# A selective scan on one core: the z projection goes into the unit that uses it, and the order tables around the silu block are set anew

## The reference

```python
def step(h, inp):
    d_t, B_t, C_t, u_t = inp
    h = h * jnp.exp(d_t[..., None] * A) + (d_t * u_t)[..., None] * B_t[:, None, :]
    y = jnp.einsum('bcn,bn->bc', h, C_t)
    return (h, y)

def _mamba_layer(x, Wi, cw, cb, Wx, Wdt, bdt, Alog, Dp, Wo):
    xz = jnp.einsum('bld,ed->ble', x, Wi)
    xin, z = jnp.split(xz, 2, axis=-1)
    xin = _silu(_causal_conv(xin, cw, cb))
    x_dbl = jnp.einsum('blc,ec->ble', xin, Wx)      # dt_raw, Bm, Cm
    delta = jax.nn.softplus(jnp.einsum('blr,cr->blc', dt_raw, Wdt) + bdt)
    y = _selective_scan(delta, Bm, Cm, xin, A, Dp)  # the scan over time of step()
    y = y * _silu(z)
    return jnp.einsum('blc,dc->bld', y, Wo)

for i in range(DEPTH):                              # 8 layers, 16 states, 512 inner channels
    x = x + _mamba_layer(x, W_in[i], ...)
```

## Time and profile before

| | us |
|---|---|
| median of 3 runs | 7655.07 |
| range of the runs | 7652.78 to 7655.28 |
| the profiled execution | 7654.07 |
| its span, first to last instruction | 7652.3 |
| DVE busy in the span | 6625.8 (87%) |
| PE busy | 6888.8 (90%) |
| ACT busy | 6410.1 (84%) |
| POOL busy | 5895.9 (77%) |

### The profile page before, as it was taken

How to read it: one execution, slowest core, us unless ns; L and a number is a source line. 1 busy time by engine, 2 the same in 40 slices (tenths; PEclk the granted TensorE clock), 3 DMA queues, 4 the chain that set the end, 5 groups by cost and what they waited for, 6 DMA issues and landing times. The chain is left out here.

```text
span 7652.3 us, 143629 instructions
## 1 busy us (share of the span) xinstructions
PE 6888.8 (90%) x39999; PEld 4756.2 (62%) x39999; DVE 6625.8 (87%) x6510; ACT 6410.1 (84%) x10314; POOL 5895.9 (77%) x4917
## 2 busy tenths in 40 slices
PE   6979999999999999999999999999999999999997
PEld 4646666666666666666666666666666666666665
DVE  3259988988998898889889988988998898899888
ACT  1258888888888888888988888888888888888987
POOL 2148887888888788888888888888888788888875
PEclk9989999999999999999999999999999999999998
DMA  4111111111111111111111111111111111111112
GB/s 163 34 43 39 41 40 47 43 40 40 42 47 42 40 39 47 44 40 39 41 47 44 40 39 42 47 43 39 41 48 43 39 40 42 45 44 40 40 39 92
DMA packets 222613, 352.40 MB, mean 46 GB/s; under 512 B 43856, under 2 KB 78448, under 8 KB 221712
## 3 DMA queue, kind: packets, MB, share of 16 engines
q1 hardware_dynamic: 218048, 332.70, 14.8%
q0 software_dynamic: 3792, 10.38, 0.4%
HBM read 325.00 MB, written 17.98 MB: 45 GB/s over the span
## 5 line engine op out<-in xcount | busy, mean ns | idle before, releaser
L897 POOL TENSOR_TENSOR drive<-du,brep 128x512 f32<-128x512 f32 x4096 | 5537.7, 1382 | 702.9 <-DVE du L1140 461.2
L936 ACT ACTIVATE prod<-ps_r,cT 128x512 f32<-128x512 f32 x4096 | 2860.8, 700 | 344.2 <-PE ps_r L1244 341.9
L929 ACT ACTIVATE ps_d<-delta,cur 128x512 f32<-128x512 f32 x4096 | 2896.9, 710 | 252.6 <-DVE state L1090 241.4
L1244 PE MATMUL ps_r<-ident,state 128*128 128x128 f32 x16384 | 2543.4, 278 | 402.3 <-ACT prod L936 153.2
L1090 DVE TENSOR_TENSOR_SCAN state<-ps_d,carry,drive 128x512 f32<-128x512 f32 x2048 | 2500.5, 1262 | 283.6 <-ACT ps_d L929 283.4
L1090 DVE TENSOR_TENSOR_SCAN state<-ps_d,drive 128x512 f32<-128x512 f32 x2048 | 2404.4, 1206 | 329.1 <-ACT ps_d L929 309.0
L1251 PE MATMUL ps_y<-ident,prod 128*128 128x128 f32 x16384 | 2459.5, 274 | 28.1 <-ACT prod L936 25.8
L1244 PEld LDWEIGHTS ps_r<-ident,state 128*128 128x128 f32 x16384 | 1829.5, 141 | 849.9 <-ACT prod L936 416.3
L1251 PEld LDWEIGHTS ps_y<-ident,prod 128*128 128x128 f32 x16384 | 1923.4, 141 | 668.6 <-issue 584.2
L1291 PE MATMUL ps_r<-xm,w_inz_sb 128*128 128x512 f32 x1024 | 506.9, 618 | 48.6 <-ACT prod L936 48.6
L1283 PE MATMUL ps_r<-xm,w_inx_sb 128*128 128x512 f32 x1024 | 510.2, 621 | 35.7 <-ACT prod L936 28.1
(11 more groups left out here) (144 smaller groups left out, 4653.4 us busy)
## 6 DMA issues: line engine op xcount, KB each, us to landing
brep<-bc_dram SPq DMA_DIRECT2D x1024, 256.0 KB, 3.2
w_sb<-w SPq DMA_DIRECT2D x8, 1024.0 KB
w_all<-w SPq DMA_DIRECT2D x8, 1024.0 KB, 11.5
xb<-xs_dram SPq DMA_DIRECT2D x39, 128.5 KB, 2.1
w_all<-x SPq DMA_DIRECT2D x4, 1024.0 KB, 9.4
w_inx_sb<-w_in SPq DMA_DIRECT2D x8, 512.0 KB, 4.1
w_inz_sb<-w_in SPq DMA_DIRECT2D x8, 512.0 KB, 4.9
w_out_sb<-w_out SPq DMA_DIRECT2D x8, 512.0 KB, 3.9
```

The source lines that it names most:

```text
L897: nc.gpsimd.tensor_tensor(drive[:, k % DRIVE, :], du[:, j, :], brep[:, n % BREP, :], ALU.mult).then_inc(drive_set, 1)
L929: nc.scalar.activation(ps_d[:, k % 2, :], delta[h][:, j, :], ACT.Exp, scale=cur[h][:, a:a + 1]).then_inc(decay_set, 1)
L936: nc.scalar.activation(prod[:, t, :], ps_r[:, item_place(U, h, kind, item), :], ACT.Copy, scale=cT[(h + 1) % 2 if item[1] == "prev" else h ...
L1244: last = nc.tensor.transpose(out[:, j * P:(j + 1) * P], state[STATE_IN[n]][:, j, t * P:(t + 1) * P], ident[:])
```

## The change

- Z0 to Z3 are projected, and read by ACT, in the unit that uses them (`own` and `in_z`), at places (0,1), (1,3), (2,3) and (3,3), not in the unit before at (10,3) to (14,0). SP's load of the next layer's z weights moves from the unit before the last of a layer into the last one; POOL's `mask_x` waits for Z3 of its own unit.
- The silu block moves from (4,1) to (5,0).
- The places of BOOST go from 4 to 8, and those of REST from 4 to 8: as many places have two decays, and as many none.
- Most other table entries move by one to eight places: the dt chain (DT0 to DT3, exp, ln, softplus) about two places later in its middle, O0 from (4,0) to (4,3), O1 from (5,1) to (6,2), the two tests for overflow from step 1 to steps 2 and 3.

The amount of computation is the same.

```diff
-RING_AT = {'CNT': (3, 2), 'O0': (4, 0), 'O1': (5, 1), 'XD': (4, 1), 'BC': (7, 3), 'DT0': (6, 0), 'DT1': (6, 2), 'DT2': (8, 1), 'DT3': (9, 2), 'Z0': (10, 3), 'Z1': (11, 2), 'Z2': (13, 2), 'Z3': (14, 0), 'X0': (5, 0), 'X1': (8, 3), 'X2': (10, 1), 'X3': (14, 3), 'C3': (17, 0)}
-SILU_AT = (4, 1)
+RING_AT = {'CNT': (3, 1), 'O0': (4, 3), 'O1': (6, 2), 'XD': (5, 0), 'BC': (8, 1), 'DT0': (6, 0), 'DT1': (8, 0), 'DT2': (10, 0), 'DT3': (10, 2), 'Z0': (0, 1), 'Z1': (1, 3), 'Z2': (2, 3), 'Z3': (3, 3), 'X0': (5, 2), 'X1': (9, 1), 'X2': (11, 1), 'X3': (14, 3), 'C3': (17, 0)}
+SILU_AT = (5, 0)
...
-MARK_AT = [(1, 0), (1, 2)]
+MARK_AT = [(2, 3), (3, 2)]
...
-SOFT_AT = [(7, 3), (8, 3), (9, 1), (10, 1), (10, 3), (11, 1), (14, 1), (14, 2)]
-CONV_AT = [(5, 3), (6, 1), (6, 3), (7, 2), (10, 0), (11, 0), (12, 0), (12, 1), (15, 1), (17, 3), (18, 0), (18, 1)]
+SOFT_AT = [(9, 0), (9, 3), (10, 2), (11, 0), (11, 1), (11, 2), (14, 3), (15, 3)]
+CONV_AT = [(6, 2), (6, 3), (7, 0), (7, 3), (10, 0), (10, 3), (11, 3), (12, 0), (15, 3), (16, 2), (19, 0), (20, 2)]
...
-BOOST_AT = [(5, 2), (7, 0), (13, 2), (15, 3)]
-REST_AT = [(4, 3), (7, 1), (14, 0), (15, 2)]
+BOOST_AT = [(1, 0), (1, 3), (2, 0), (4, 0), (5, 3), (6, 2), (6, 3), (13, 2)]
+REST_AT = [(0, 0), (2, 2), (3, 3), (4, 3), (6, 1), (7, 0), (7, 2), (15, 1)]
...
-                nc.scalar.activation(zs[hf][:, j, :], ps_r[:, item_place(U, h, kind, f"Z{j}"), :], ACT.Copy).then_inc(ring_act, 1)
+                nc.scalar.activation(zs[h][:, j, :], ps_r[:, item_place(U, h, kind, f"Z{j}"), :], ACT.Copy).then_inc(ring_act, 1)
...
+                        for j in range(CB):
+                            if (n, t) == RING_AT[f"Z{j}"]:
+                                in_z(U, h, kind, it, j)
```

47 lines of the change are left out of this document (25 added, 22 removed).

## The result

| | before | after |
|---|---|---|
| median of 4 runs, us | 7655.17 | 7871.78 |
| range, us | 7652.78 to 7663.62 | 7850.84 to 7909.03 |
| profiled execution, us | 7654.07 | 7909.03 |
| its granted clock of PE, mean | 0.994 | 0.974 |

The changed kernel is slower: ratio 1.0286, 95% interval 1.0264 to 1.0308. The forecast was 7620 and the range 7540 to 7720, so both the sign and the range were missed: the result is 217 us above the kernel before, 252 above the forecast and 152 above the top of the range.

A forecast was written before the change was run, and what follows sets the result against it. DVE was taken as the bound, running or short of a decay. Idle of 6.0 + 1.7 + 1.85 + 0 = 9.55 against 10.1 us saves 0.55 over 63 units, 35 us: 7620 us, range 7540 to 7720.

The forecast's parts named there:

- What bounds the kernel: DVE runs or is short of a decay; a change can win at most its 10.1 us idle a unit.
- The block, three places later: DVE's gap at the moved silu block: 6.0 us idle a unit against 5.54, O0's wait inside it.
- Catching up behind it: Scans behind the silu block, with O1 at (6,2): 1.7 us idle a unit against 4.27, a win of 2.6.
- Steps 7 and 8: ACT's extra reads and exponential delay scans 36 and 37: 1.2 plus 0.65, 1.85 us idle; bounds 0 and 2.4.
- Steps 0 to 4: PE takes four z projections with 1.3 us to spare: 0 us idle taken, bounds 0 and 2; count tightest.
- rival 2: PE overfull in steps 0 to 4, late decays cost 1 to 2 us a unit: 7715 us; chance 0.25.
- At no cost: SP's z-weights load holding up B transfers, and POOL's halo wait, are covered; DVE never waits for drives: 0.
- A rule on bubbles: The repeated 5.5 us gap at the block means too few buffers; `ps_d` stays at two, so it stays whole.
- Rival 1: No net change: `ps_d` sets the block's gap, gains behind it are lost at step 8; 7640 to 7670; chance 0.20.
- Rival 3: ACT reaches step 8 with a decay in hand, the 1.85 us there go: 7500 us; chance 0.15.

The follow-up runs named there:

- half_before: Kernel before with drives of 256 instead of 512 columns, half of POOL's work left out, result incomplete; 7566.55 us (ratio 0.9882).
- mark_o1: Changed kernel with overflow tests back at (1,0) and (1,2), and SP's out-weights load moved behind the B transfers for steps 8 to 15; 7679.86 us.
- half_after: Changed kernel with drives of 256 instead of 512 columns, half of POOL's work left out, result incomplete; 7616.66 us (ratio 0.9946).
- before_mark: Kernel before with only the two overflow tests moved, from (1,0) and (1,2) to (2,3) and (3,2); 7673.86 us (ratio 1.0024).
- mark_inz: Changed kernel with overflow tests back at (1,0) and (1,2), and SP's z-weights load moved behind the B transfers for steps 8 to 15; 7727.86 us.
- z_later: As mark_o1, with Z2 moved from (2,3) to (3,2) and Z3 from (3,3) to (4,1), behind the count; 7756.36 us (ratio 1.0133).
- z_alone: Changed kernel's code with all tables of the kernel before, except Z0 to Z3 at (0,1), (1,3), (2,3), (3,3); 8008.15 us (ratio 1.0461).

## Why the prediction was wrong

**What bounds the kernel.** DVE runs or is short of a decay: still true. What I took from it, that a change can act only on the 10.1 us of idle time, was the error. DVE's busy time is no fixed quantity; it has some 2 us a unit of standing behind POOL in it already in the kernel before, and 3.8 more in the changed one (own time a unit, which is the sum over DVE's instructions from the start of one to the start of the next, less the idle time: 100.75 before, 98.9 in half_before, 104.56 after). The page showed POOL busy 77% of the span, and one and the same instruction took from 685 to 1757 ns, 1142 in the median. In units 8 to 59 the test takes 1.11 to 1.19 us every time, so the sign was not a spread from unit to unit but a median far above the shortest. I looked at neither.

**The block, three places later** (6.0 us): right. In mark_o1 the wait for O0 and the gap before (5,3) are 4.28 + 1.71 = 5.99 (means of even and odd units). They are split otherwise than I put it: O0 is the later of the two, and the decays hide behind it.

**Catching up behind it** (1.7): right; before (6,0) and (7,0) stand 1.10 + 0.61 = 1.71.

**Steps 7 and 8** (1.85): right in place, before scans 36 and 37, and a little less, 1.11 + 0.34 = 1.45. The terms of its first part give 2.33 + 0.7 - 2.32 = 0.71, where I wrote 0.8; nothing hangs on it.

**Steps 0 to 4** (0, bounds 0 and 2): the value was wrong, the bounds held. DVE waits 1.6 us for the count at (3,3) in mark_o1 (1.48 in even units, 1.74 in odd). I had named the count as the tightest point and then taken 0. This is rival 2's mechanism at the size I gave it, 1 to 2 us; it did not come before a decay of step 3 or 4, but before the count, whose projection stands behind three of z on PE. The 1.3 us to spare were not there: PE is busy for 24.76 of 25 us ahead of the count.

The sum of idle time in mark_o1 is thus 6.0 + 1.7 + 1.45 + 1.6 = 10.8 against 10.1 before; had the count been free, it would have been 9.2, near the 9.55 of the forecast.

**The durations of DVE's moved instructions** (priced at nothing): the step that failed. Moving the tests, the taps and the halo changed which of them meet POOL in a row of drives. It cost 147 to 152 us by the tests alone. The prediction took POOL only as a source of drives, never as a neighbour that DVE has to wait for inside an instruction. That it is POOL, half_after shows; why the drives pass DVE over in the changed kernel and not at the same place in before_mark, no run does.

**At no cost** (SP and POOL): half wrong. The cover of the z load held, as mark_inz shows by changing nothing. But I looked only at SP's instruction that the diff moves. SP's wait for O1, whose line the diff doesn't touch, moved with O1's table entry, and the transfers of B stand behind it: 40 to 44 us, and the waits of DVE for drives that I had named as a sign of being wrong. A moved item moves what waits for it too.

**A rule on bubbles**: no kernel shortened the gap behind the block; it is 5.54 us before, 6.0 in mark_o1, 6.8 in z_later. The Trainium skill, page "Perfetto Trace Analysis", section "Optimization Strategy", says that such a gap can mean too few buffers; they were left at two and the gap stayed, so the trace agrees as far as it goes. No run changed their number.

**The rivals.** Rival 1 (no net change) describes the change best once POOL's part is out: in their plain units half_after and half_before differ by 0.06 us (even) and 0.34 (odd). Rival 2 had the right sign, and its place and its size a unit (1 to 2 us) came true, but it is 1.6 x 63 = 100 of 217 us at most, and in the changed kernel less, since the long test hides part of the wait for the count (0.8 us a unit). The rule that I set against it, to judge PE's room by its weight loads (the Trainium skill, page "Perfetto Trace Analysis", section "Identifying the Most-Contended Engine"), misled: PEld is busy for 60 to 62% of the span in z_alone and mark_o1 too, and PE is late in both. In the 25 us ahead of the count PEld went from 15.64 to 16.15 us, while PE went from 21.98 to 24.76. (The section also names MFU, the share of peak arithmetic, which I did not work out.) Rival 3 is refuted: both gaps ahead of scans 36 and 37 are there. None of them had DVE's own time in it.

## What to carry to other kernels

Before moving a VectorE instruction in a kernel in which GpSimd is busy most of the time, look at that instruction's shortest, median and longest duration by source line, not at its mean. An instruction that works from SBUF alone is no fixed cost: put it where GpSimd waits, as at (4,2), where the tap took 0.7 us in all 52 units of the changed kernel, or try the neighbouring places, since here one place was worth 35 to 80 us. When an item moves in an order table, list every engine that waits for it, DMA queues first, and what stands behind that wait; the engine that stalls in the end may be three steps away. And when the time of a changed kernel spreads between runs where that of the old one didn't, look for an instruction with two lengths.

## What the runs showed of the hardware

- A DVE instruction from SBUF that comes up within a row of GpSimd instructions can stand over several of them: 4.14 us for a test of 0.66, 3.22 us for a tap of 0.72, up to 5.95 us at worst. It then waits for more than the one drive of 1.25 us that runs, and ends some 0.6 us behind the row (unit 26 of the changed kernel). Where it gets in at once it waits for the rest of one drive, 1.69 us for the test in unit 10, and the next drive takes 1.73 us instead of 1.27.
- With equal timing to 0.01 us the outcome differs: the test that comes up 0.13 to 0.14 us into a drive took 1.69 us in unit 10 and 4.20 in unit 16. There are 41 long tests and 11 short ones in units 8 to 59 of one execution of the changed kernel, and times of one kernel from 7851 to 7909 us where the four runs of the kernel before lie within 11.
- A fall of the clock, 3.4 us at 1.2 GHz, went with 0.8 us more of a unit near scan 35 (mark_o1) and with none near scan 58 (z_alone).
- Halving the work of POOL, which is busy for 77% of the span and for which DVE never waits by the view of waits, made the kernel before 1.2% faster. DVE's own time fell by 1.85 us a unit (100.75 to 98.9), while its idle time grew by 0.5 (10.1 to 10.6).
